# Two-layer macaron block on one core: weights laid out by the host, shared tiles moved forward, one product for the queries

## The chip, the cores and the metric

One core of one Trainium2 chip runs the whole program. The metric is device time in microseconds (us) of one execution, taken over several runs; the profile shows one more execution. The engines are named as in the profile: PE (TensorE), PEld (its weight loads), DVE (VectorE), ACT (ScalarE), POOL (GpSimd) and SP (SyncE, which only issues DMAs here).

## The reference, cut to what matters

Tokens are (2, 1024, 128) in f32. The block is FFN, attention, FFN, each on a layer norm of x and added to x:

```python
x = x + 0.5 * ffn(layernorm(x))
x = x + attn(layernorm(x))
x = x + 0.5 * ffn(layernorm(x))        # the same weights again
# attn, 16 heads of 8 columns
v = x @ w_v + v_b
q = (x @ w_q + q_b) @ w_k.T + k_b      # the keys are x itself
probs = softmax(causal(q @ x.T / sqrt(8)));  out = (probs @ v) @ c_proj_w + c_proj_b
# ffn: one shared expert and the 2 best of 7 routed ones, hidden width 352
expert(h, g, u, d) = (silu(h @ g.T) * (h @ u.T)) @ d.T
w = normalised top-2 of softmax(h @ wr.T + rb)
out = expert(h, sg, su, sd) + sum_e w[e] * expert(h, rg[e], ru[e], rd[e])
```

## The kernel before, in words

**Precision.** Every large product is made of three fp32r products: each operand is split into a high part (a copy to fp32r, by ACT) and a low part (operand minus high part, by DVE), and high x high, high x low and low x high are summed in PSUM. Weights need the same split (`wall` holds both parts of g, u and d for 8 experts; `small` those of attention).

**Weights.** g, u and d arrive as the reference has them, and both operands of a product must have the summed index on partitions. So PE transposes them: `weights_pe` (L1417) makes three transposes for one of 24 groups (8 experts x g, u, d) into a PSUM bank, `weights_hi_act` (L1454) copies the high part, `weights_lo_dve` (L1476) subtracts. Eleven groups (`TP_FIRST`) come ahead of the first tile, the other 13 one for each of the first 13 steps of the FFN. `weights_small_pe` (L1409) transposes w_k and the router's weights.

**Start.** 2048 tokens are four chunks (c) of 512. DVE makes statistics, POOL the reciprocal deviations (`norm_rstd_pool`), ACT the normalised rows z (`norm_z_act`), PE transposes them (`norm_tr_pe`, L548), ACT and DVE split (`norm_hi_act`, `norm_lo_dve`). `logits_pe` (L581) makes the router's logits. For each half (h) of the tokens, `router_dve` (L634) is a chain of 14 short DVE instructions that finds the two best experts, `places_pe` (L695) counts with two products, `places_dve` (L743) ends in `slots`, the rows to which POOL scatters each token (`sort_pool`, L1151: 16 indirect DMAs for a half, each followed by `pause_pool`, a memset). SP then reads tiles of sorted rows back (`rows_load_sp`, L1222): batch 0 to 2 (10 tiles) need the first half, batch 3 onward the second.

**FFN.** `ffn_pe`, `ffn_act` and `ffn_dve` (L961, L1016, L1125) walk 54 jobs of 128 tokens: 13 shared tiles (whose rows need no sorting), 38 routed tiles, 3 shared tiles. Step s makes the up products of job s, the transposes of job s-1 and the down products of job s-2. Each engine has one queue in program order. What else is done in a step is written in tables by hand (L2090 on): `FRONT_` ahead of the job's own work, `BETWEEN_` behind the up products or silu, `BEHIND_` at the end. `AWAKE` adds filler products (`busy_pe`) behind the up products of steps 0 and 1. POOL scatters the results (`scatter_pool`), and they are read back and mixed into x with the routing weights.

**Attention.** Queries take two products: `q1_pe` (x w_q), split with bias by `q1_act`/`q1_dve` (L1530, L1572), then `q_pe` (with w_k, L1519) and `q_act`/`q_dve`. Chunks 0 and 1 are done in steps 45 to 52 of the first FFN, chunks 2 and 3 inside the prologue of attention (`SECOND_PE`, `SECOND_DVE`, L1729), where DVE takes 54 maxima of score tiles (the ring) ahead of the first exponential. Then come 8 groups of 4 heads, and the second FFN.

```python
961 def ffn_pe(K, f):
963     for step in range(NQ + 2):
964         if f == 0 and TP_FIRST + step < NTP:
965             weights_pe(K, TP_FIRST + step)
...
974             if f == 0 or step > 0:
975                 up_pe(K, f, step, bases.get(step, 0))
```

Of the kernel before, what the change touches and what calls it, by code (L numbers as in the profile page):

```python
# [120 lines left out]
AWAKE = [{0: 2, 1: 3}, {}]  # L121
# [130 lines left out]
N_BANKS = (5, 4)  # L252
RING, SLOTS, O_BANK, END_BANK = (2, 5, 7, 3), (0, 1, 4), 6, 5
MID_N_BANK, Q1_BANK, Q_BANK, V_BANK = (7, 2, 0, 1), (3, 3, 4, 0), (7, 2, 6, 4), (7, 3, 1, 0)
# [3 lines left out]
TP_GROUPS = [(w, x) for x in range(EXPERTS) for w in ("g", "u", "d")]  # L258
NTP = len(TP_GROUPS)
TP_FIRST = 11  # L260
TP_BANK = [(0, 1, 2, 3, Z_BANK)[m % 5] if m < TP_FIRST else Z_BANK for m in range(NTP)]
# [6 lines left out]
TP_FREE = [max((p + 1 for p in range(m) if TP_BANK[p] == TP_BANK[m]), default=0) for m in range(NTP)]  # L268
# [3 lines left out]
N_CONST2 = 7  # L272
# [11 lines left out]
def place_memory(K, ctx):  # L284
# [19 lines left out]
    for w in ("q", "k", "v", "p"):  # L304
        for part in ("h", "l"):
            K.small[w + part] = sb(f"w{w}_{part}", [P, EMB], F32R)
# [5 lines left out]
    K.b_k = sb("b_k", [P, 1])  # L312
    K.b_v = sb("b_v", [P, EMB])
# [33 lines left out]
    with ExitStack() as s:  # L347
        zt = [sb(f"zt_{part}", [P, TOKENS], F32R, scope=s) for part in ("h", "l")]
        with ExitStack() as s2:
# [18 lines left out]
            with ExitStack() as s3:  # L368
                K.nat = {w: sb(f"nat_{w}", [P, EXPERTS, 3, EMB], scope=s3) for w in ("g", "u")}
                K.nat["d"] = sb("nat_d", [P, EXPERTS * HID + 32], scope=s3)  # L370
                K.nat_attn = sb("nat_attn", [P, 3 * EMB], scope=s3)
                K.nat_proj = sb("nat_proj", [P, EMB], scope=s3)
                K.nat_route = sb("nat_route", [P, P], scope=s3)
                rows = sb("rows", [32, 2, CHUNK], scope=s3)
                K.rows0, K.rows1 = rows[:, 0, :], rows[:, 1, :]
            with ExitStack() as s3:
# [3 lines left out]
                with ExitStack() as s4:  # L380
# [38 lines left out]
    with ExitStack() as s:  # L419
# [19 lines left out]
    K.ld = {n: sem(f"ld_{n}") for n in ("nat", "nat2", "small", "bias", "const", "out")}  # L439
# [3 lines left out]
    K.tp_pe, K.tp_hi, K.tp_lo = sem("tp_pe"), sem("tp_hi"), sem("tp_lo")  # L443
# [17 lines left out]
            ("q1", "q1f", "q1h", "q1l", "q", "qf", "qh", "ql", "v", "vev", "vb", "init",  # L461
             "ring", "taken", "mm", "sp", "ex", "mk", "pv", "oev", "vg", "ready", "nm", "rs", "vi", "og", "otr", "oh", "ol", "op", "bp", "xup")}
# [85 lines left out]
def norm_tr_pe(K, k, c):  # L548
# [10 lines left out]
    if c > 1:  # L559
# [456 lines left out]
def ffn_act(K, f):  # L1016
    for step in range(NQ + 1):
        if f == 0 and TP_FIRST + step < NTP:
            weights_hi_act(K, TP_FIRST + step)
# [131 lines left out]
def sort_pool(K, f, g):  # L1151
# [4 lines left out]
    if f == 0 or g % TT > 0:  # L1156
# [111 lines left out]
def start_sp(K):  # L1268
# [15 lines left out]
    e.dma_start(K.nat["d"][:, HID:EXPERTS * HID].rearrange("p (e i) -> p e i", i=HID), K.down_r.rearrange("e h i -> h e i"))\
     .then_inc(K.ld["nat2"], 16)
# [27 lines left out]
def start_act(K):  # L1313
# [4 lines left out]
    e.dma_start(K.nat_route[0:ROUTED, :], K.route_w).then_inc(K.ld["small"], 16)  # L1318
# [7 lines left out]
def start_pool(K):  # L1326
# [31 lines left out]
    e.memset(K.nat["d"][:, EXPERTS * HID:], 0.0).then_inc(K.consts2, 1)  # L1358
# [995 lines left out]
```

## Time and profile before

| | |
|---|---|
| median of 3 runs (lowest to highest) | 596.37 us (594.8 to 597.38) |
| the profiled execution | 592.31 us, its span 590.6 us |
| PE busy, share of the span | 543.8 us, 92% |
| DVE busy | 453.5 us, 77% |
| ACT busy | 331.0 us, 56% |
| POOL busy | 254.8 us, 43% |
| first FFN, silu of job 0 to silu of job 53 | 36.8 to 173.9 us |
| prologue of attention to its first exponential | 178.8 to 219.4 us |
| second FFN, silu of job 0 | from 453.4 us on |

The span runs from the first to the last instruction; the 1.7 us beside it lie around them. The timeline view gives start and duration of each instruction, and in brackets how long its engine had been idle before it and what released it. "Granted clock" (PEclk) is what the throttle allowed, as a share of full speed; the pace of the products themselves shows which of its two levels (1.2 or 2.4 GHz) PE runs at.

### The profile page before, as it was taken

Reading aid. Unit: us, or ns where it says so; the run is one execution under the profiler, and the core shown is the slowest. Engines: PE = TensorE matmul, PEld = TensorE weight load, DVE = VectorE, ACT = ScalarE, POOL = GpSimd, SP = SyncE. Lnnn points to the kernel's source line nnn. Section 1 sums busy time; section 2 is a strip of 40 time slices with the busy share of each in tenths; the row PEclk is TensorE's granted clock in tenths of the full one; section 3 lists DMA queues with packets and bytes.
Section 4 is the critical chain, followed back from the end, with each engine's and each line's share of the span. In section 5 each row is a group of like instructions: output and inputs, shape, how many; then the busy total and the mean of one; then the engine's idle time right before and its main releaser. Section 6 shows DMA issues by size and latency. Waiting matters only on the chain. (4 is left out here: it accounts for less than half of the span.)

```text
span 590.6 us, 11873 instructions
## 1 busy us (share of the span) xinstructions
PE 543.8 (92%) x3738; PEld 431.3 (73%) x3738; DVE 453.5 (77%) x1151; ACT 331.0 (56%) x701; POOL 254.8 (43%) x400
## 2 busy tenths in 40 slices
PE   1898999998895779999999999999999999999996
PEld 1778999997783546666666666666655889999995
DVE  3679868779548899797979797979564888777965
ACT  4454444446643527676767676768777434444543
POOL 7387856445342161111111212121236888864440
PEclk9999999999997989999999999999999999999997
DMA  9931435941563356222222222220000121341314
GB/s 244 290 83 38 122 80 145 234 126 48 162 197 110 114 155 162 82 87 83 88 86 84 90 80 86 86 88 10 4 2 24 32 78 52 101 110 59 107 38 113
DMA packets 46889, 58.74 MB, mean 99 GB/s; under 512 B 6183, under 2 KB 37678, under 8 KB 46062
## 3 DMA queue, kind: packets, MB, share of 16 engines
q1 hardware_dynamic: 38160, 46.77, 28.2%
q0 software_dynamic: 4480, 9.25, 4.9%
q10 hardware_dynamic: 4190, 1.98, 1.3%
q8 instruction: 33, 0.54, 0.4%
q14 instruction: 26, 0.21, 0.1%
HBM read 38.09 MB, written 28.00 MB: 112 GB/s over the span
## 5 line engine op out<-in xcount | busy, mean ns | idle before, releaser
L1771 DVE TENSOR_REDUCE mxp<-psum 128x1 f32<-128x512 f32 (+3 forms) x304 | 179.5, 655 | 30.3 <-PE psum L1617 29.4
L1830 ACT ACTIVATE probs<-psum 128x512 f32<-128x512 f32 (+1 forms) x304 | 155.1, 578 | 41.2 <-PE psum L1660 38.1
L1660 PE MATMUL psum<-queries,keys 128*128 128x512 f32 (+3 forms) x384 | 122.4, 381 | 0.5 <-DMA queries<-m_rows 0.3
L1617 PE MATMUL psum<-keys,queries 128*128 128x512 f32 (+1 forms) x304 | 115.3, 414 | 1.3 <-DVE mxp L1771 0.9
L1877 POOL TENSOR_SCALAR_AFFINE_SELECT probs<-probs 128x512 f32<-128x512 f32 x64 | 39.9, 634 | 175.5 <-ACT probs L1830 175.4
L1177 POOL DMA_INDIRECT y_rows<-ys,to_row x76 | 74.4, 979 | 81.4 <-DVE ys L1085 53.7
L996 ACT ACTIVATE silu<-psum 128x352 f32<-128x352 f32 x107 | 49.7, 464 | 102.6 <-PE psum L890 101.3
L1041 DVE TENSOR_TENSOR act<-silu,psum 128x352 f32<-128x352 f32 x107 | 55.5, 519 | 46.2 <-ACT silu L996 45.4
L1660 PEld LDWEIGHTS psum<-queries,keys 128*128 128x128 f32 x384 | 66.7, 190 | 26.7 <-ACT probs L1830 12.6
L1689 PE MATMUL psum<-probs,vg 128*32 128x512 f32 (+3 forms) x768 | 69.8, 491 | 0.4 <-POOL probs L1877 0.4
L1617 PEld LDWEIGHTS psum<-keys,queries 128*128 128x128 f32 x304 | 57.9, 193 | 15.0 <-DVE mxp L1771 4.8
L1047 DVE TENSOR_TENSOR at_l<-psum,at_h 128x384 fp32r<-128x384 f32 x108 | 59.5, 551 | 7.3 <-ACT at_h L1004 7.1
L906 PE MATMUL psum<-ident,act 128*128 128x128 f32 x324 | 53.7, 275 | 4.5 <-DVE at_l L1047 3.8
L1004 ACT CAST at_h<-psum 128x384 fp32r<-128x384 f32 x108 | 51.3, 475 | 9.1 <-PE psum L906 8.5
L888 PE MATMUL psum<-wall,zs_h 128*128 x152 | 54.0, 355 | 1.3 <-DVE zs_l L1072 1.0
L890 PE MATMUL psum<-wall,zs_l 128*128 x152 | 49.1, 323 | 0.0
L889 PE MATMUL psum<-wall,zs_h 128*128 x152 | 49.0, 323 | 0.0
L924 PE MATMUL psum<-wall,at_h 128*128 x228 | 47.6, 318 | 1.3 <-DVE ys L1085 1.3
L906 PEld LDWEIGHTS psum<-ident,act 128*128 128x128 f32 x324 | 40.9, 140 | 9.7 <-issue 4.4
L1689 PEld LDWEIGHTS psum<-probs,vg 128*32 128x32 f32 x768 | 21.1, 109 | 35.5 <-issue 21.7
L1154 POOL DMA_INDIRECT z_rows<-zrow,slots x32 | 31.2, 975 | 16.8 <-DVE slots L739 11.9
L924 PEld LDWEIGHTS psum<-wall,at_h 128*128 128x128 f32 x228 | 33.4, 190 | 2.9 <-issue 2.0
(260 smaller groups left out, 1020.5 us busy)
## 6 DMA issues: line engine op xcount, KB each, us to landing
z_rows<-q_stack SPq DMA_DIRECT2D x12, 682.5 KB, 5.2
keys<-q_stack SPq DMA_DIRECT2D x12, 512.0 KB, 10.3
keys<-k_stack SPq DMA_DIRECT2D x32, 128.0 KB, 6.3
queries<-q_stack SPq DMA_DIRECT2D x8, 512.0 KB, 6.0
zg_early<-z_rows SPq DMA_DIRECT2D x44, 65.0 KB, 1.9
yc<-y_rows SPq DMA_DIRECT2D x10, 256.0 KB, 3.9
zg_late<-z_rows SPq DMA_DIRECT2D x32, 65.0 KB, 2.1
k_stack<-zt_h SPq DMA_DIRECT2D x8, 256.0 KB, 3.0
```

The lines of the kernel that those rows point to most:

```text
L888: e.matmul(dst, zh, weight(K, base, hi, HID), start=True, stop=False)
L906: ins = e.transpose(bank(K, at_bank(f, q))[:, k * P:(k + 1) * P], K.act[:, q % 2, k * P:(k + 1) * P], K.ident[:, :])
L924: e.matmul(dst[:, 0:2 * EMB], K.at_h[:, q % 2, k * P:(k + 1) * P], weight(K, base, DN + 2 * k * EMB, 2 * EMB), start=(k == 0), stop=False, ...
L1004: e.copy(K.at_h[:, q % 2, :], bank(K, at_bank(f, q))[:, 0:ACOLS]).then_inc(s["hi"], 1)
L1041: e.tensor_tensor(act, silu, up, ALU.mult).then_inc(s["act"], 1)
L1047: e.tensor_tensor(K.at_l[:, q % 2, :], bank(K, at_bank(f, q))[:, 0:ACOLS], K.at_h[:, q % 2, :].bitcast(F32), ALU.subtract)\
L1177: e.indirect_dma_start(K.y_dram[f], bass.IndirectOffsetOnAxis(ap=K.to_row[:, j:j + 1], axis=0), K.ys[:, j % RING_Y, :], None).then_inc(K.y ...
L1617: ins = e.matmul(dst, K.queries[u][:, i * P:(i + 1) * P], K.keys[u][:, heads[0]:heads[-1] + 1, k0 * P:(k0 + nb) * P], start=True, stop=Tru ...
L1660: ins = e.matmul(slot(K, u, d, n)[:, m * (q1 - q0):(m + 1) * (q1 - q0)], K.keys[v][:, j, kt * P:(kt + 1) * P], K.queries[v][:, q0:q1], sta ...
L1689: ins = e.matmul(bank(K, O_BANK)[32 * j:32 * j + 32, q0 - half * CHUNK:q1 - half * CHUNK], K.vg[:, kt, j, :], probs_of(K, n)[:, j, :], sta ...
L1771: e.tensor_reduce(K.mxp[:, heads[0]:heads[-1] + 1, i, which], scores, AX.X, ALU.max).then_inc(K.A["taken"], 1)
L1830: e.activation(probs_of(K, product)[:, heads[0]:heads[-1] + 1, :], src, ACT.Exp, scale=SCALE).then_inc(K.A["ex"], 1)
```

## The change: what it does, and the diff

The host hands the weights over already transposed (and d padded with zero rows to 384), so the 24 groups of PE transposes and the two small ones are gone. The splits remain, in ten larger pieces: the 3 shared ones (352 or 384 elements a partition) on ACT and DVE ahead of the first tile; four (g and u of experts 1 to 3 and 4 to 7: 1056 and 1408 elements) with the high part on ACT and the low part **on POOL, ahead of the sort**; three (d, 896 elements each) on ACT and DVE in steps 0 to 3. The first tile follows the logits of chunks 0 and 1 at once. Transposes and splits of chunks 2 and 3, their logits, the places of the first half, and the second half's router (steps 6 and 7), places (step 10), segments and lists (up to step 15) move into the shared steps. The filler products and the pauses of the first FFN's sort are gone. w_q w_k^T is formed once by PE (`query_weights_pe`), with a combined bias, and queries take one product. SP loads the experts' weights with 6 DMAs instead of 14, in the same order.

```diff
-AWAKE = [{0: 2, 1: 3}, {}]
+AWAKE = [{}, {}]
...
+WEIGHTS = [(w, slice(0, 1)) for w in ("g", "u", "d")] + \
+          [(w, slice(x0, x1)) for w in ("g", "u") for x0, x1 in ((1, 4), (4, EXPERTS))] + [("d", k) for k in range(3)]
+SHARED_WEIGHTS = 3
+POOL_WEIGHTS = [3, 4, 5, 6]
+LATE_WEIGHTS = [7, 8, 9]
...
 def norm_tr_pe(K, k, c):
...
-    if c > 1:
+    if k == 0 and c == 3:
+        e.wait_ge(K.NS[k]["lo"], c)
+    elif c > 1:
         e.wait_ge(K.NS[k]["lo"], c - 1)
...
 def rows_tr_pe(K, f, b):
...
-        e.wait_ge(K.tp_lo, NTP)
+        e.wait_ge(K.w_lo, len(WEIGHTS) - len(POOL_WEIGHTS))
+        e.wait_ge(K.w_lo_pool, len(POOL_WEIGHTS))
...
 def ffn_pe(K, f):
...
-        if f == 0 and TP_FIRST + step < NTP:
-            weights_pe(K, TP_FIRST + step)
         if f == 0 and step == 0:
-            e.wait_ge(K.tp_lo, TP_FIRST)
+            e.wait_ge(K.w_lo, SHARED_WEIGHTS)
...
 def sort_pool(K, f, g):
...
-    if f == 0 or g % TT > 0:
+    if f == 1 and g % TT > 0:
         pause_pool(K, f == 1 and t < HALF)
...
+    e.dma_start(K.nat["g"][:, 0, :], K.gate_s).then_inc(K.ld["shared"], 16)
+    e.dma_start(K.nat["u"][:, 0, :], K.up_s).then_inc(K.ld["shared"], 16)
+    e.dma_start(K.nat["d"][:, :, 0, :], K.down_s).then_inc(K.ld["shared"], 16)
+    e.dma_start(K.nat["g"][:, 1:, :], K.gate_r).then_inc(K.ld["g"], 16)
+    e.dma_start(K.nat["u"][:, 1:, :], K.up_r).then_inc(K.ld["u"], 16)
+    e.dma_start(K.nat["d"][:, :, 1:, :], K.down_r).then_inc(K.ld["d"], 16)
...
+def query_weights_pe(K):
+    e = K.nc.tensor
...
+    e.matmul(bank(K, Y_BANK)[:, 0:EMB], K.nat_attn[:, 0:EMB], K.nat_attn[:, EMB:2 * EMB], start=True, stop=True,
+             skip_group_check=True)
+    e.matmul(bank(K, Y_BANK)[:, EMB:EMB + 1], K.nat_attn[:, EMB:2 * EMB], K.b_q[:, :], start=True, stop=True,
+             skip_group_check=True).then_inc(K.A["qk"], 1)
...
+def weights_lo(K, e, m, done):
+    w, src, hi, lo = (WEIGHTS[m][0],) + weights_of(K, m)
+    e.wait_ge(K.w_hi, m + 1)
+    if w != "d":
+        e.tensor_tensor(lo, src, hi.bitcast(F32), ALU.subtract).then_inc(done, 1)
+    else:
+        e.scalar_tensor_tensor(lo, src, 0.5, hi.bitcast(F32), ALU.mult, ALU.subtract).then_inc(done, 1)
...
 def q_pe(K, c):
...
-    three(K, e, bank(K, Q_BANK[c]), (K.small["kh"][:, :], K.small["kl"][:, :]), (K.q1_h[:, :], K.q1_l[:, :]))\
+    three(K, e, bank(K, Q_BANK[c]), (K.small["qh"][:, :], K.small["ql"][:, :]), (K.zt_h[1][:, cols], K.zt_l[1][:, cols]))\
         .then_inc(K.A["q"], 1)
-def q1_act(K, c):
...
-def q1_dve(K, c):
...
-SECOND_PE = {11: (("n_tr", 2),), 14: (("q1", 2),), 15: (("n_tr", 3),), 19: (("q1", 3),), 21: (("q", 2),),
-             25: (("q", 3),), 26: (("v", 2),), 28: (("v", 3),)}
+SECOND_PE = {11: (("n_tr", 2),), 15: (("n_tr", 3), ("q", 2)), 20: (("q", 3),), 21: (("v", 2),), 23: (("v", 3),)}
...
-FRONT_PE = {4: (("places", 1),), 45: (("n_tr", 0),), 46: (("q1", 0),), 47: (("n_tr", 1),), 48: (("q", 0), ("q1", 1)),
-            50: (("q", 1),), 51: (("v", 0),), 52: (("v", 1),)}
-BETWEEN_ACT = [{46: (("q1", 0),), 48: (("q", 0), ("q1", 1)), 50: (("q", 1),)}, {}]
+FRONT_PE = {9: (("places", 1),), 45: (("n_tr", 0),), 46: (("q", 0),), 47: (("n_tr", 1),), 48: (("q", 1),),
+            50: (("v", 0),), 51: (("v", 1),)}
+BETWEEN_ACT = [{0: (("hi0", 2),), 1: (("hi0", 3),), 46: (("q", 0),), 48: (("q", 1),)}, {}]
...
+FRONT_DVE = {4: (("segments", 0),), 5: (("lists", (0, 0)), ("lists", (0, 1)), ("lists", (0, 2)), ("lists", (0, 3))),
+             6: (("router", (1, 0)),), 7: (("router", (1, 1)),), 10: (("places", 1),), 11: (("segments", 1),),
+             12: (("lists", (1, 0)),), 13: (("lists", (1, 1)),), 14: (("lists", (1, 2)),), 15: (("lists", (1, 3)),)}
+BEHIND_DVE = [{0: (("query", 0),), 1: (("weights_lo", LATE_WEIGHTS[0]),), 2: (("weights_lo", LATE_WEIGHTS[1]),), 3: (("weights_lo", LATE_WEIGHTS[2]),), 13: (("small", 0),), 22: (("weights", 0),), 40: (("mix", 0),), 41: (("n_stats", 0),), 42: (("mix", 1),), 43: (("n_stats", 1),), 44: (("n_lo", 0),),
...
+BETWEEN_PE = [{0: (("tr0", 2),), 1: (("places", 0), ("tr0", 3)), 3: (("logits0", 2),), 4: (("logits0", 3),)}, {1: (("proj_tr", 2), ("proj_tr", 3)), 4: (("logits", 2), ("logits", 3)), 6: (("places", 1),)}]
+BETWEEN_DVE = [{0: (("lo0", 2),), 1: (("lo0", 3),)}, {4: (("router", (1, 0)),), 6: (("places", 1),)}]
...
         @block.gpsimd
         def _(e):
             start_pool(K)
             for c in range(NCH):
                 norm_rstd_pool(K, 0, c)
+            for m in POOL_WEIGHTS:
+                weights_lo(K, e, m, K.w_lo_pool)
             sort_part_pool(K, 0, 0)
             sort_part_pool(K, 0, 1)
...
+def laid_out(name, a):
+
+    if name == "attn_c_attn_w":
+        a = np.concatenate([a[:, 0:EMB].T, a[:, EMB:2 * EMB].T, a[:, 2 * EMB:]], axis=1)
+    elif name in ("ffn_sg", "ffn_su", "ffn_wr"):
+        a = a.T
+    elif name in ("ffn_rg", "ffn_ru"):
+        a = a.transpose(2, 0, 1)
+    elif name in ("ffn_sd", "ffn_rd"):
+        rows = np.moveaxis(a, -1, 0)
+        padded = np.concatenate([rows, np.zeros_like(rows[0:3 * P - HID])])
+        a = np.moveaxis(padded.reshape((3, P) + rows.shape[1:]), 0, 1)
+    return np.ascontiguousarray(a)
```

## Rows read from the trace of the kernel before

**Rows 1.** Windows: length, busy us of each engine, granted clock, DMA share, GB/s
```profile
15.00:20.00 5.00, 4.92 (x23) 4.95 (x24) 1.65 (x6) 3.32 (x9) 1.23 (x2) 1.00 1.05 280
...
34.60:37.90 3.30, 3.30 (x12) 2.29 (x11) 1.19 (x3) 2.24 (x3) 2.97 (x5) 1.00 0.15 45
37.90:45.00 7.10, 7.10 (x51) 6.05 (x50) 6.04 (x21) 3.16 (x7) 6.44 (x10) 1.00 0.11 38
...
158.00:166.00 8.00, 6.46 (x37) 5.89 (x36) 3.84 (x8) 3.57 (x9) 2.11 (x2) 0.79 0.59 183
```

**Rows 2.** Timeline, ACT and DVE, 14.6 to 25.2 us: normalised rows, the first half's router chain
```profile
14.66 3.41 ACT L531 ACTIVATE zrow<-x,mr_neg,rstd 128x128 f32<-128x128 f32 x8
...
18.73 0.22 DVE L628 TENSOR_TENSOR r_log<-psum,rb_row 128x64 f32<-128x64 f32 x1 [3.20 <-PE psum L596]
...
21.89 0.22 DVE L672 TENSOR_TENSOR r_sel<-r_c,r_m 128x64 bf16<-128x64 f32 x1
...
24.99 0.17 DVE L739 CAST slots<-d_slot 128x16 int32<-128x16 f32 x1
```

**Rows 3.** Timeline, ACT: a cast from SBUF of 512 elements
```profile
150.80 0.62 ACT L1539 CAST q_h<-q_f 128x512 fp32r<-128x512 f32 x1
```

**Rows 4.** Groups by form, POOL: times run, busy us, mean ns, idle before
```profile
L1164 POOL MEMSET idle<- 128x384 bf16 x68 | 29.5, 434 | 0.0
L1556 POOL TENSOR_TENSOR v_all<-v_all,b_v 128x128 f32<-128x128 f32 x16 | 7.2, 481 | 9.2 <-ACT v_all L1546 9.1
L2075 POOL TENSOR_TENSOR x<-x,b_p 128x512 f32<-128x512 f32 x4 | 4.9, 1266 | 0.0
```

**Rows 5.** Source L1779, DVE: shortest, median and longest ns of eight
```profile
L1779 DVE TENSOR_TENSOR mm_hl<-nmax,mm_hl x8: 191/193/1195, 214.1 to 418.5; 128x32 fp32r<-128x32 f32 x8
```

**Rows 6.** Timelines of DVE and of POOL, 212.7 to 215.3 us
```profile
214.08 1.20 DVE L1779 TENSOR_TENSOR mm_hl<-nmax,mm_hl 128x32 fp32r<-128x32 f32 x1
...
212.74 2.48 POOL L2075 TENSOR_TENSOR x<-x,b_p 128x512 f32<-128x512 f32 x2
```

**Rows 7.** Timeline, ACT: silu of jobs 3 and 12, first FFN
```profile
45.09 0.46 ACT L996 ACTIVATE silu<-psum 128x352 f32<-128x352 f32 x1 [0.49 <-PE psum L890]
...
70.82 0.47 ACT L996 ACTIVATE silu<-psum 128x352 f32<-128x352 f32 x1 [0.48 <-PE psum L890]
```

**Rows 8.** Timeline, ACT: silu of shared jobs 4, 9, 51 and 53, second FFN
```profile
468.80 0.46 ACT L996 ACTIVATE silu<-psum 128x352 f32<-128x352 f32 x1 [0.38 <-PE psum L890]
...
484.50 0.46 ACT L996 ACTIVATE silu<-psum 128x352 f32<-128x352 f32 x1 [0.60 <-issue]
...
575.39 0.46 ACT L996 ACTIVATE silu<-psum 128x352 f32<-128x352 f32 x1 [1.20 <-PE psum L890]
...
580.01 0.46 ACT L996 ACTIVATE silu<-psum 128x352 f32<-128x352 f32 x1 [1.48 <-PE psum L890]
```

**Rows 9.** Timeline, ACT: silu of jobs 46, 50 and 53, first FFN
```profile
149.72 0.46 ACT L996 ACTIVATE silu<-psum 128x352 f32<-128x352 f32 x1 [0.31 <-PE psum L890]
...
164.84 0.46 ACT L996 ACTIVATE silu<-psum 128x352 f32<-128x352 f32 x1 [3.12 <-PE psum L890]
...
173.90 0.46 ACT L996 ACTIVATE silu<-psum 128x352 f32<-128x352 f32 x1 [1.08 <-PE psum L890]
```

**Rows 10.** Timeline, DVE: in the prologue of attention
```profile
199.37 0.68 DVE L1577 TENSOR_TENSOR q_l<-q_f,q_h 128x512 fp32r<-128x512 f32 x1
...
201.32 0.69 DVE L1771 TENSOR_REDUCE mxp<-psum 128x4 f32<-128x512 f32 x1 [0.67 <-PE psum L1617]
```

**Rows 11.** Timeline: POOL's last scatter of the sort, SP's and PE's batch 3
```profile
76.87 0.96 POOL L1154 DMA_INDIRECT z_rows<-zrow,slots  x1 [0.16 <-issue]
...
79.32 0.88 SPq L1238 DMA_DIRECT2D zg_early<-z_rows  x2
...
90.94 0.40 PE L947 MATMUL psum<-ident,zg_early 128*128 128x128 f32 x2
```

**Rows 12.** The page, DMA issues: count, KB each, median us to landing
```profile
zg_early<-z_rows SPq DMA_DIRECT2D x44, 65.0 KB, 1.9
```

More of the change, by code:

```diff
@@ L251 @@
 AT_BANKS = (5, 7)
-N_BANKS = (5, 4)
+N_BANKS = (5, 4, 6, 6)
 RING, SLOTS, O_BANK, END_BANK = (2, 5, 7, 3), (0, 1, 4), 6, 5
[L254 to L261, printed above, removed]
+MID_N_BANK, Q_BANK, V_BANK = (7, 2, 0, 1), (7, 2, 6, 4), (7, 3, 1, 0)
+WEIGHTS = [(w, slice(0, 1)) for w in ("g", "u", "d")] + \
[3 more added lines that the diff above has]
+LATE_WEIGHTS = [7, 8, 9]
 RING_LAST = RING0[LAST] + RINGN * (GROUPS - 1)
@@ L267 @@
 R_BANKS = [[R_BANK, R_BANK], [EARLY_BANKS[0], R_BANK]]
-TP_FREE = [max((p + 1 for p in range(m) if TP_BANK[p] == TP_BANK[m]), default=0) for m in range(NTP)]
 N_CONST = 6
-N_CONST2 = 7
+N_CONST2 = 6
 N_SPARES = 4
@@ L303, in place_memory @@
     K.small = {}
-    for w in ("q", "k", "v", "p"):
+    for w in ("q", "v", "p"):
         for part in ("h", "l"):
@@ L435, in place_memory @@
     K.psum = ctx.enter_context(K.nc.psum_tensor("psum", [P, 8, CHUNK], F32))
-    K.ld = {n: sem(f"ld_{n}") for n in ("nat", "nat2", "small", "bias", "const", "out")}
+    K.ld = {n: sem(f"ld_{n}") for n in ("shared", "g", "u", "d", "small", "bias", "const", "out")}
     K.ld_x = [sem(f"ld_x{b}") for b in range(BATCH)]
@@ new lines, in small_sources, with weights_of @@
+def small_sources(K):
+    return [("v", K.nat_attn[:, 2 * EMB:]), ("p", K.nat_proj[:, :])]
+def weights_of(K, m):
+    w, part = WEIGHTS[m]
+    wall = K.wall[:, :].rearrange("p (x c) -> p x c", c=WCOLS)
+    if w != "d":
+        hi, lo = (GH, GL) if w == "g" else (UH, UL)
+        return K.nat[w][:, part, :], wall[:, part, hi:hi + HID], wall[:, part, lo:lo + HID]
+    down = wall[:, :, DN:].rearrange("p x (k a m) -> p x k a m", a=2, m=EMB)
+    if m < SHARED_WEIGHTS:
+        return K.nat[w][:, :, 0, :], down[:, 0, :, 0, :], down[:, 0, :, 1, :]
+    return K.nat[w][:, part, 1:, :], down[:, 1:, part, 0, :], down[:, 1:, part, 1, :]
@@ new lines, in weights_hi_act @@
+def weights_hi_act(K, m):
+    e, w = K.nc.scalar, WEIGHTS[m][0]
+    src, hi, _ = weights_of(K, m)
+    if m < SHARED_WEIGHTS:
+        e.wait_ge(K.ld["shared"], 16 * 3)
+    else:
+        e.wait_ge(K.ld[w], 16)
+    if w == "d":
+        e.activation(hi, src, ACT.Copy, scale=0.5).then_inc(K.w_hi, 1)
+    else:
+        e.copy(hi, src).then_inc(K.w_hi, 1)
+def weights_lo(K, e, m, done):
+    w, src, hi, lo = (WEIGHTS[m][0],) + weights_of(K, m)
+    e.wait_ge(K.w_hi, m + 1)
+    if w != "d":
+        e.tensor_tensor(lo, src, hi.bitcast(F32), ALU.subtract).then_inc(done, 1)
+    else:
+        e.scalar_tensor_tensor(lo, src, 0.5, hi.bitcast(F32), ALU.mult, ALU.subtract).then_inc(done, 1)
@@ L1856, in attn_act @@
     e = K.nc.scalar
-    e.wait_ge(K.A["ready"], 1)
+    e.wait_ge(K.A["ready"], 2)
     for c in range(2, NCH):
@@ L2142, in late_act @@
         norm_z_act(K, 2, c)
+    elif step == "hi0":
+        norm_hi_act(K, 0, c)
+    elif step == "weights":
+        weights_hi_act(K, c)
     elif step == "tanh":
@@ L2173, in late_dve @@
         norm_z_dve(K, 2, c)
+    elif step == "lo0":
+        norm_lo_dve(K, 0, c)
+    elif step == "query":
+        query_weights_dve(K)
+    elif step == "small":
+        weights_small_dve(K)
+    elif step == "weights_lo":
+        weights_lo(K, K.nc.vector, c, K.w_lo)
     elif step == "norm_lo":
@@ L2235, in _ @@
             logits_pe(K, 0, 0, 1)
[L2236 to L2245 removed]
+            query_weights_pe(K)
             ffn_pe(K, 0)
```

220 lines of the change are left out of this document (62 added, 158 removed).

## Prediction

> **What bounds the kernel now.** I read the windows first, then the timeline of the first 80 us engine by engine, then the waits. Up to 34.6 us no tile is computed: PE transposes weights and makes logits, ACT and DVE split. From the first tile on PE is nearly always busy [rows 1], except between the first FFN and attention (6.46 of 8 us in 158 to 166 us). So the change can pay in three places: the start, that passage, and the prologue of attention, where DVE is the bound. From the first loop of attention to the end nothing that it edits is on the path, and I carry the sum of the three through unchanged. A change of under 0.5% (3.0 us) can't be told from none here.
>
> **Start: what goes.** The 24 transpose groups go; eleven stood ahead of the tiles, and the filler products of steps 0 and 1 as well. If nothing else came, PE would reach the first up products right behind the logits, whose results DVE takes up at 18.73 us [rows 2], against 34.6 us.
>
> **Start: what comes on POOL.** ACT ends the normalised rows at 14.66 + 3.41 = 18.07 us [rows 2]. Three shared casts come ahead (1.15 us, at under 0.4 us each after the cast of 512 in 0.62 us [rows 3]), so 19.2. The first large cast (1056 elements, 1056 x 0.62 / 512 = 1.28) ends at 20.5, all four by 25.2. POOL subtracts the low parts. Its nearest rows are a two-input product of 128 elements, 0.48 us, and of 512, 1.27 us [rows 4]: 2.04 ns an element. So 1056 cost 2.4 us, 1408 cost 3.1, all four 11.0 us, without a gap because ACT is ahead. DVE meanwhile runs the router's chain (18.73 to 22.11 us) and the places (slots ready at 25.16) [rows 2], short instructions, nearly all with two SBUF inputs.
>
> Do the two engines get in each other's way? L1779, a DVE subtraction of 32 elements with both inputs in SBUF, takes 191 to 193 ns, and once 1195 [rows 5]. That once, it starts at 214.08 and ends at 215.28, just when POOL's x + b_p ends (212.74 + 2.48 = 215.22) [rows 6]. It stood for the rest of POOL's instruction. I take this as the rule for the chain: each DVE instruction with two SBUF inputs that meets a running POOL subtraction waits for its end. Four waits are needed (L659, L664 with L665, L667, L672), as many as there are POOL instructions, since POOL's next is queued when DVE's one has passed. POOL ends at 20.5 + 11.0 + 0.6 for DVE's turns = 32.1, the router at 32.35 instead of 22.11, 10.2 us late, and the slots at 35.4 instead of 25.16. From below: no waits, nothing; from above: 11 us, all of POOL.
>
> The Trainium skill, SBUF — State Buffer, "Who interferes with whom", speaks against the change: a DVE instruction with two SBUF inputs and a GpSimd instruction that reads SBUF share one read interface, and the loser is held for the whole instruction. By it all four waits come; by the one row alone I would know only of one, and with one wait (2.4 us) the sum would be some 7.8 us better. The trace agrees as far as it goes, 1195 ns against 193.
>
> **Who waits for DVE.** `places_dve` is queued on DVE ahead of job 0's product. PE makes up 0 and 1 by 24 us and then stands at `places_pe`. From 35.4 on: job 0's product 0.5, low part of chunk 2 0.7, transposes of chunk 3 1.1, of job 0 0.6, up of job 2 1.7, transposes of job 1 0.6, down of job 0 1.9, up of job 3 1.4 and silu's wait 0.4, since PE comes out of a pause and its instructions start about every 0.28 us, as in 34.6 to 37.9 us, not every 0.14 as behind it [rows 1]. Silu of job 3 falls on 44.3, against 45.09 [rows 7]: **0.8 us** gained. Without the waits the slots come at 26.7 (PE reaches the places at 24), and 9.5 us would be gained.
>
> **Steps 3 to 12.** Before, nine jobs take 70.82 - 45.09 = 25.7 us [rows 7], each with a transpose group. Without one a shared job takes (580.01 - 575.39) / 2 = 2.31 us [rows 8]. But logits of chunks 2 and 3, router, places and segments of the second half now lie in these steps. The second FFN has the same work in jobs 4 to 9, 15.7 us for five [rows 8], 4.15 above 5 x 2.31. For the segments and lists of the first half I add 1.5 (below 0, above 3). 9 x 2.31 + 4.15 + 1.5 = 26.4: **0.7 lost**. The late weights (896 elements, three on ACT and DVE, about 1 us each) lie beside PE's slow steps 0 to 3.
>
> **Between FFN and attention.** Jobs 46 to 53 take 173.90 - 149.72 = 24.2 us [rows 9]. Gone are six products of 512 columns, four ACT casts (0.62 [rows 3]) and two DVE subtractions (0.68). Where q and q1 met in step 48, 2.6 us of ACT stood ahead of the transposed activations; 1.3 remain. Followed job by job the silus come 0.5, 1.4, 2.7 and at last 3.3 us earlier. Bounds: 1.3 (one pair of casts) and 4.0 (24.2 less seven jobs at 2.31 and 4.0 us of other products). I take **3.3**.
>
> **Prologue.** DVE is busy nearly throughout; it loses two subtractions of 0.68 and the 0.67 us for which it waits behind the second step of the queries [rows 10]. With v moved five places forward, POOL's x + b_p ends ahead of L1779, another 1.0 [rows 5]. Together **3.0**, bounds 1.4 and 3.7.
>
> **Covered.** The query weights cost PE two small products, about 0.5 us, in the time in which it waits anyway; if the waits on DVE don't come they cost 0.5. SP has fewer, larger DMAs, and clears the keys behind the row loads as before.
>
> **Sum.** 0.8 - 0.7 + 3.3 + 3.0 = 6.4 us. The profiled execution took 592.31 us (span 590.6 and 1.7 around it), which gives 585.9; it lies 4.1 below the median of the runs, 596.37. I predict from the median: **590.0 us**.
>
> **Rivals.**
> 1. *DVE isn't held.* Only one row shows the hold, and other two-input instructions beside short POOL work took their usual time. Then 9.5 - 0.7 - 0.5 + 3.3 + 3.0 = 14.6: 581.8 us. Chance 0.15.
> 2. *Some waits.* DVE gets two instructions through at each turn: two POOL instructions fewer in the way, some 5 us more: 585 us. Chance 0.12.
> 3. *The second half's sort is late.* Its places move from step 5 to step 10: five jobs at 2.86 [rows 7] behind 53.5 (last scatter at 76.87, 15 at 1.56 ahead of it [rows 11]), so 67.7. Without pauses 16 scatters take 1.12 each (0.96 and a gap of 0.16): 85.6. SP loads 1.5 later, as 79.32 stands to 77.83 [rows 11], two issues 0.9, landing 1.9 [rows 12]: 89.9, and batch 3 is wanted at 90.9. One us is left. If the scatters without the memset (0.43 [rows 4]) need 1.56 all the same, rows come 6 us late and the gain is 0.4: 596 us. Chance 0.08.
> 4. *Slower: PE stays at its lower level.* In 15 to 20 us PE was busy 4.92 of 5 us with narrow products at the slow pace though 1.00 was granted, and it rose only behind fillers [rows 1]. Now there are none, and PE has a pause ahead. At twice the interval a shared job takes about 4.2 us, 1.9 more; from four jobs on the whole gain is lost, over jobs 3 to 12 it is 19: 603 us. Against it: up products of 352 columns follow one another closely as soon as jobs run. Chance 0.07.
>
> **The numbers.** My forecast has 0.58, of which 0.09 gain under 3 us (the bounds of the steps at their worst). Faster by over 0.5%: 0.49 + 0.15 + 0.12 = 0.76; within: 0.09 + 0.08 = 0.17; slower: 0.07. The range runs from 580 (rival 1 and a little) to 595 (the lower bounds, most of rival 3); rival 4 and the edges are left out.
>
> **What would show it.** In the changed profile: L659 to L672 with durations of 2 to 3 us and POOL's four subtractions at 2.4 and 3.1; the first half's slots at 35 us (27 in rival 1); silu of job 3 near 44; jobs 3 to 12 in 26.4; jobs 46 to 53 in 21; first exponential 6 us earlier; no wait on batch 3 (one of 6 us in rival 3). Small router instructions at 0.22 us throughout would prove the start wrong; shared jobs of 4 us, rival 4.

## The result and the profile after

The changed kernel took 615.49 us (median of four runs, 612.52 to 617.52); the kernel before took 596.88 in the runs beside it. Ratio 1.031, 95% interval 1.0247 to 1.0373: **slower by 18.6 us**, where 6.4 us of gain were forecast. The profiled execution has a span of 615.7 us against 590.6.

The page of the changed kernel, its head, TensorE's busy tenths and granted clock in 40 slices, and the shares of the chain that ended last:

```profile
span 615.7 us, 11594 instructions
...
PE   1473946999899588999999999999999899989996
...
PEclk9877877999999697999999999999999989999998
...
PE 63%; DVE 13%; issue 10%; another core or an unknown queue 5%; POOL 3%; ACT 3%; DMA 2%; SPq 1%; DVEq 0%; POOLq 0%
```

PE has holes in slices 2 to 7, up to 108 us. 15% of the chain is time for which the profile can name no cause ("issue" and "another core or an unknown queue"; 5% in e10 below, which runs almost the same program without the trouble). Where it lies is shown by silu, ACT's first instruction of each job. The changed kernel, timeline of ACT, jobs 3, 4, 5, then 12 and 13, then 46 and 53:

```profile
41.48 0.46 ACT L1000 ACTIVATE silu<-psum 128x352 f32<-128x352 f32 x1 [0.61 <-PE psum L892]
44.64 0.46 ACT L1000 ACTIVATE silu<-psum 128x352 f32<-128x352 f32 x1 [1.49 <-issue]
55.72 0.46 ACT L1000 ACTIVATE silu<-psum 128x352 f32<-128x352 f32 x1 [7.37 <-remote]
...
80.30 0.46 ACT L1000 ACTIVATE silu<-psum 128x352 f32<-128x352 f32 x1 [3.16 <-issue]
97.23 0.46 ACT L1000 ACTIVATE silu<-psum 128x352 f32<-128x352 f32 x1 [9.40 <-remote]
...
175.26 0.47 ACT L1000 ACTIVATE silu<-psum 128x352 f32<-128x352 f32 x1 [0.31 <-PE psum L892]
...
196.17 0.47 ACT L1000 ACTIVATE silu<-psum 128x352 f32<-128x352 f32 x1 [1.57 <-issue]
```

Job 3 came 3.6 us earlier than before [rows 7]. Jobs 3 to 12 then took 38.8 us instead of 25.7, and job 13 another 16.9 (before 3.8). Jobs 46 to 53 took 20.91 against 24.2 [rows 9], as forecast. The lost time lies in two stretches, and in both POOL scatters without a pause: 37.75 to 58.4 us and 75.33 to 95.3 us, one scatter each 1.26 us. The changed kernel, waits in 43 to 60 us (engine, line waited for, us in total, times, longest):

```profile
ACT silu L1000 <- remote: 7.4, 1, 7.4
PEld psum L908 <- issue: 7.1, 2, 5.5
PE psum L908 <- issue: 5.1, 1, 5.1
ACT at_h L1008 <- remote: 4.4, 2, 2.8
POOL z_rows L1154 <- issue: 3.7, 12, 0.3
DVE act L1043 <- issue: 3.6, 1, 3.6
DVE at_l L1049 <- issue: 2.5, 2, 1.8
```

PE, ACT and DVE all stand, though the instructions they depend on have ended; I call this a stall. POOL alone goes on. The second FFN, whose code is unchanged, lost 4.9 us too (jobs 1 to 53 in 126.8 instead of 121.9).

The start went nearly as forecast. The changed kernel, DVE's router chain (each line has a number two higher than in the kernel before), POOL's four subtractions and its first scatter:

```profile
19.91 2.33 DVE L659 TENSOR_TENSOR r_sel<-r_c,zrow 128x64 bf16<-128x64 f32 x1
22.28 3.10 DVE L661 SCALAR_TENSOR_TENSOR r_w<-r_sel,r_log 128x64 f32<-128x64 bf16 x1
...
25.66 2.08 DVE L666 TENSOR_TENSOR r_c<-r_w,r_p 128x64 f32<-128x64 f32 x1
27.66 3.12 DVE L667 TENSOR_TENSOR r_d<-r_m,r_p 128x8 f32<-128x8 f32 x1
...
34.37 0.17 DVE L741 CAST slots<-d_slot 128x16 int32<-128x16 f32 x1
```
```profile
19.71 5.59 POOL L1463 TENSOR_TENSOR wall<-nat_g,wall 128x1056 fp32r<-128x1056 f32 x2 [3.62 <-ACT wall L1456]
25.24 5.52 POOL L1463 TENSOR_TENSOR wall<-nat_u,wall 128x1056 fp32r<-128x1056 f32 x2
37.75 1.22 POOL L1154 DMA_INDIRECT z_rows<-zrow,slots  x1 [6.99 <-issue]
```

### The profile page after: what moved, and what is told of

Its sections match the earlier page's. It is cut to its first block, busy times and chain, and to the rows that moved or that the text cites. A ratio compares the mean times of both kernels' runs of the same rounds, so it can differ in the third digit from the quotient of the medians.

```text
span 615.7 us, 11594 instructions
## 1 busy us (share of the span) xinstructions
PE 538.0 (87%) x3646; PEld 424.5 (69%) x3646; DVE 452.3 (73%) x1129; ACT 323.9 (53%) x678; POOL 252.6 (41%) x371
## 4 chain that ended last, share of the span: by engine, by line
PE 63%; DVE 13%; issue 10%; another core or an unknown queue 5%; POOL 3%; ACT 3%; DMA 2%; SPq 1%; DVEq 0%; POOLq 0%
PE psum L1631 12%; PE psum L1588 11%; PE psum L1660 10%; PE psum L890 4%; PE psum L892 4%; PE psum L908 4%; PE psum L929 4%; PE psum L891 4%; PE psum L932 2%; DVE mxp L1741 2%; PE psum L1591 2%; DVE at_l L1049 1%; POOL z_rows L1154 1%; PE psum L1616 1%
## 5 line engine op out<-in xcount | busy, mean ns | idle before, releaser
L908 PE MATMUL psum<-ident,act 128*128 128x128 f32 x324 | 55.9, 283 | 15.0 <-issue 5.5
L890 PE MATMUL psum<-wall,zs_h 128*128 x152 | 55.1, 363 | 9.9 <-issue 9.1
L1008 ACT CAST at_h<-psum 128x384 fp32r<-128x384 f32 x108 | 51.3, 475 | 16.9 <-PE psum L908 6.9
L891 PE MATMUL psum<-wall,zs_h 128*128 x152 | 50.1, 329 | 0.0
L1660 PEld LDWEIGHTS psum<-probs,vg 128*32 128x32 f32 x768 | 21.1, 109 | 35.6 <-issue 21.4
L1154 POOL DMA_INDIRECT z_rows<-zrow,slots x32 | 31.5, 984 | 33.0 <-DVE slots L741 16.9
L890 PEld LDWEIGHTS psum<-wall,zs_h 128*128 128x128 f32 x152 | 29.6, 195 | 10.6 <-issue 10.3
```

The costliest lines, as they stand in the source:

```text
L890: e.matmul(dst, zh, weight(K, base, hi, HID), start=True, stop=False)
L891: e.matmul(dst, zh, weight(K, base, lo, HID), start=False, stop=False)
L908: ins = e.transpose(bank(K, at_bank(f, q))[:, k * P:(k + 1) * P], K.act[:, q % 2, k * P:(k + 1) * P], K.ident[:, :])
L1660: ins = e.matmul(bank(K, O_BANK)[32 * j:32 * j + 32, q0 - half * CHUNK:q1 - half * CHUNK], K.vg[:, kt, j, :], probs_of(K, n)[:, j, :], sta ...
```

## The experiments

Sixteen kernels, and two programs run once more, in five sets. The kernels of one set share a chip and the runs of the kernel before; each set had another chip (its number is in the table; that of the result isn't on record). All results first, because their order by set turned out to be the finding. "Stalls" means that PE, ACT or DVE stands for 3 us or more, with no releaser that the trace can name, while POOL scatters; the longest such stand in a trace marked "no" is 2.7 us.

| set, chip | kernel before, us | run | us | ratio, 95% interval | stalls |
|---|---|---|---|---|---|
| result | 596.9 | changed kernel | 615.5 | 1.031, 1.025 to 1.037 | yes |
| 1, chip 7 | 593.1 | e1 pauses back | 595.9 | 1.0039, 1.0007 to 1.0071 | no |
| 1, chip 7 | | e2 before, no pauses | 593.6 | 1.0002, 0.997 to 1.0034 | no |
| 1, chip 7 | | e3 lock off | 591.1 | 0.9963, 0.9931 to 0.9995 | no |
| 1, chip 7 | | e4 short pauses | 591.3 | 0.997, 0.9932 to 1.0007 | no |
| 2, chip 2 | 600.9 | e5 lock off, no pauses | 613.7 | 1.0207, 1.0158 to 1.0257 | yes |
| 2, chip 2 | | e6 pauses in first half | 612.8 | 1.0188, 1.0124 to 1.0251 | second half |
| 2, chip 2 | | e7 each fourth pause | 616.4 | 1.0247, 1.0184 to 1.031 | yes |
| 2, chip 2 | | e8 before, 20 pauses ahead | 628.9 | 1.0456, 1.0389 to 1.0522 | yes |
| 3, chip 4 | 594.3 | e9 before, 20 memsets ahead | 593.9 | 0.9984, 0.9948 to 1.0021 | no |
| 3, chip 4 | | e10 changed, 20 memsets ahead | 591.4 | 0.9957, 0.9929 to 0.9985 | no |
| 3, chip 4 | | e11 lock off, short pauses | 589.0 | 0.9903, 0.987 to 0.9937 | no |
| 3, chip 4 | | e12 and fillers | 589.5 | 0.9899, 0.9865 to 0.9934 | no |
| 4, chip 6 | 593.4 | e13 20 memsets behind | 592.2 | 0.9979, 0.9946 to 1.0012 | no |
| 4, chip 6 | | e14 10 memsets | 591.7 | 0.9927, 0.9897 to 0.9956 | no |
| 4, chip 6 | | e15 40 memsets | 591.7 | 0.9944, 0.99 to 0.9988 | no |
| 4, chip 6 | | e16 wait alone | 591.3 | 0.9981, 0.994 to 1.0021 | no |
| 5, chip 15 | 595.1 | e17 changed kernel again | 614.3 | 1.0319, 1.0276 to 1.0362 | yes |
| 5, chip 15 | | e18 = e2 again | 624.4 | 1.0494, 1.0458 to 1.0529 | yes |

**Set 1: pauses and lock, one at a time.** "Lock" is short for POOL's subtractions holding DVE. e1, the changed kernel with the pauses back; e2, the kernel before with the opposite edit:

```diff
-    if f == 1 and g % TT > 0:
+    if f == 0 or g % TT > 0:
```

> The changed kernel with the pauses between the scatters of the first FFN back (a memset of 0.43 us behind each of the 32), nothing else undone. Theory A (without pauses POOL's scatters hold up the other engines; the two stretches of stalls, 45 to 59 us and 77 to 98 us, go): the first FFN's jobs 3 to 13 take the 29.5 us of the kernel before instead of 55.8, and the time is 585 to 593 us, near 589. Rival B (the stalls come of what else was changed: rows that land late, the layout's transfers, the missing fillers' clock): the stalls stay, 608 us or more. A time between, 595 to 605 us, would say that both take part.

> The kernel before without the pauses between the scatters of the first FFN, nothing else changed. Theory A: the same stalls appear in it while POOL scatters, 610 to 622 us. Rival B: the pauses were only time of POOL, whose sort has slack: 590 to 598 us, no change that can be told. Rival C (as in the prediction, the sort ends earlier by 16 x 0.6 us and feeds the first routed tiles): up to 3 us faster.

e3 is e1 with the four subtractions moved from POOL to DVE, in BEHIND_DVE[0] (POOL_WEIGHTS, renamed MID_WEIGHTS, remains for ACT's casts):

```diff
-            for m in POOL_WEIGHTS:
-                weights_lo(K, e, m, K.w_lo_pool)
...
+ 4: (("weights_lo", 3),), 5: (("weights_lo", 4),), 8: (("weights_lo", 5),), 9: (("weights_lo", 6),),
```

> As the kernel with the pauses back, and the low parts of the four large weights taken from POOL and put on DVE, behind its work of jobs 4, 5, 8 and 9. Theory A with the lock (POOL's 11.1 us of subtractions held DVE's router chain, for which PE stood 8.7 us): against the kernel with the pauses back 5 to 9 us faster, near 582 us, the four router operations back at 0.23 us. Rival D (the 8.7 us are covered by something else that is late, or the four subtractions of some 1.2 us now make DVE late in jobs 4 to 9): within 2 us of it.

e4 is e1 with a memset of 32 columns in each pause of the first FFN:

```diff
-        pause_pool(K, f == 1 and t < HALF)
+        pause_pool(K, f == 1 and t < HALF, 32 if f == 0 else PAUSE)
```

> As the kernel with the pauses back, with a memset of 32 columns instead of 384 in each pause of the first FFN, so that a scatter comes each 1.25 to 1.35 us instead of 1.57, with POOL's wait for its own memset kept. Theory A1 (it is the rate of the scatters that holds the others up): the stalls come back in good part, 600 us or more. Theory A2 (it is that POOL never stands still between two scatters; any wait of its own frees the others): as with the full pause, within 2 us of it.

e1 had no stalls, but at 595.9 us it was not the 589 of theory A, and above its 593. e2 had none either: on this evidence the pauses protect nothing in the kernel before. I took that at first for an effect of the program. e4 was 4.7 us faster than e1, where the theory without stalls (A2) had at most 2. e3, DVE's router chain and slots, then POOL's first scatter:

```profile
20.30 0.23 DVE L659 TENSOR_TENSOR r_sel<-r_c,zrow 128x64 bf16<-128x64 f32 x1
20.56 0.23 DVE L661 SCALAR_TENSOR_TENSOR r_w<-r_sel,r_log 128x64 f32<-128x64 bf16 x1
...
26.29 0.17 DVE L741 CAST slots<-d_slot 128x16 int32<-128x16 f32 x1
```
```profile
27.45 1.22 POOL L1153 DMA_INDIRECT z_rows<-zrow,slots  x1 [10.49 <-DVE slots L741]
```

Without POOL's subtractions the held instructions are back at 0.23 us and the slots come 8.1 us earlier than in the changed kernel. That shows the hold. The kernel gained 4.8 us against e1 (595.93 to 591.11), a little less than the 5 to 9 expected: job 3 came 8.0 us earlier than in e1 (34.60 against 42.59), but DVE makes the four subtractions now, PE waits for it, and at job 13 1.2 us of the 8.0 are left (70.99 against 72.14).

**Set 2: what the stalls need.** e5 is e3 without the pauses of the first FFN. e6 and e7 change the condition in the changed kernel, e8 adds pauses to e2 (in this order):

```diff
-    if f == 1 and g % TT > 0:
+    if f == 0 and t < HALF or f == 1 and g % TT > 0:
```
```diff
-    if f == 1 and g % TT > 0:
+    if f == 0 and t % 2 == 0 and r == 0 or f == 1 and g % TT > 0:
```
```diff
+            for _ in range(20):
+                pause_pool(K)
             sort_part_pool(K, 0, 0)
```

> The kernel with the lock off (low parts of the four large weights on DVE), without the pauses in the first FFN: the changed kernel with the lock alone undone. So far the pauses' absence cost 20 us in the changed kernel and nothing in the kernel before, at the same spacing of the scatters (1.26 us), and a scatter each 1.27 us with a short wait between stalled nobody. Theory E (the stalls need scatters without a wait between them at a place in time that the lock brought about: POOL's sort then runs 11 us later against the other engines): with the sort again beginning near 27 us no stall, 588 to 594 us. Theory F (they need scatters without a wait and something else of the changed kernel: its program or its layout in SBUF): the stalls stay, 604 us or more.

> The changed kernel with the pauses in the first half of the first FFN's sort alone. If each half's stalls come of its own scatters: the stretch at 45 to 59 us is free, the one at 77 to 98 us stays with some 12 us, and the time is 602 to 609 us. If the second stretch was only a consequence of the first: 593 to 599 us.

> The changed kernel with one pause behind each fourth scatter of the first FFN. If the stalls build up over a row of scatters and one wait of POOL's clears them: within 3 us of the kernel with all pauses (596). If each scatter without a wait costs its share: some three quarters of the 20 us stay, 609 us or more.

> The kernel before without the pauses, and 20 of them in a row ahead of the first half's sort, so that its scatters begin some 11 us later (near 37 to 38 us), as in the changed kernel. Theory E (place in time): the stalls appear, 604 us or more. Theory F (the changed program or layout): no stall, 593 to 600 us, the later sort being covered in part.

All four stalled. The most useful is e6. Its waits in 43 to 64 us (first half, with pauses) and in 66 to 84 us (second half, without):

```profile
ACT silu L1000 <- PE psum L892: 9.3, 6, 1.9
ACT silu L1000 <- issue: 3.0, 2, 1.5
```
```profile
ACT silu L1000 <- remote: 5.4, 1, 5.4
...
DVE act L1043 <- issue: 4.1, 1, 4.1
```

Within one execution the half with pauses runs (jobs 3 to 11 in 21.9 us; in e10, which didn't stall, 21.4), the half without stalls (job 11 to 13 in 27.2 us, e10 8.1). Its time, 612.8 us, lies above the 602 to 609 expected; the kernel before took 600.9 there. One pause in four (e7) doesn't protect. e8 did not do what I meant: its pauses ended before the slots were ready, so the scatters began at 26.56 us, as in e2 at 26.43, and at the same pace. Yet e2 had run free and e8 stalled. I looked for the cause in POOL's program, the only difference between the two kernels, and passed over the other one, the chip.

**Sets 3 and 4: the place in the program.** Short memsets of 2 columns, which only move what stands behind them in POOL's program: e9 in e2 ahead of the sort; e10, e14 and e15 in the changed kernel ahead of POOL's subtractions (20, 10, 40); e13 behind the sort.

```diff
+            for i in range(20):
+                e.memset(K.idle[:, 2 * i:2 * i + 2], 0.0).then_inc(K.rested, 1)
+                K.rests += 1
```

> The kernel before without the pauses, and 20 memsets of 2 columns in POOL's program ahead of the sort: as many instructions more as in the kernel with 20 pauses ahead of it (which stalled, 1.046, although its scatters began at 26.56 us as they did without, 26.43, and came as fast), but POOL done with them by 20 us and standing for some 6 us before the first scatter. Theory P (what decides whether scatters without a wait stall the others is where in POOL's program they stand): the stalls appear, ratio to the kernel before 1.02 or more. Theory Q (it is that POOL was at work right up to the first scatter): no stall, ratio 0.995 to 1.005.

> The changed kernel with 20 memsets of 2 columns in POOL's program ahead of its four subtractions, in time in which POOL stood. Theory P: the stalls change, by several us up or down, or go (ratio 1.00 to 1.02, or 1.04 and more). Theory Q: they stay as they are, ratio 1.027 to 1.037.

> The changed kernel with the 20 memsets of 2 columns in POOL's program behind both halves of the sort instead of ahead of it. Ahead of it they took all stalls away (0.9957). If it is the place of the scatters in POOL's program (or what POOL did ahead of them): nothing changes for the 32 scatters, ratio 1.025 to 1.037, both stretches of stalls there. If it is what stands behind them or the length of the program: the stalls go, 0.993 to 1.003.

> The changed kernel with 10 memsets of 2 columns ahead of POOL's subtractions (20 took the stalls away). If any shift or any such work ahead is enough: 0.993 to 1.003. If the place matters in steps: the ratio can be that of the changed kernel, 1.02 or more, at this number.

> The changed kernel with 40 memsets of 2 columns ahead of POOL's subtractions. If such work ahead is enough: 0.993 to 1.003 as with 20. If the place matters in steps: the stalls may be back, 1.02 or more; with 10 and 20 and 0 that gives the pattern.

e16 puts a wait between the scatters of the changed kernel, on a semaphore long met (`elif f == 0: e.wait_ge(K.numbered, 1)`):

> The changed kernel with a wait between the scatters of the first FFN for a semaphore that has long been met, and no memset. If a wait in the instruction frees the others (the scatters take it in with no instruction between): no stalls, 0.993 to 1.003. If it needs an instruction of another kind, or POOL's stand for its own memset: as the changed kernel, 1.025 to 1.037.

None stalled, whatever the number or the place: a theory that needs a place can't hold when every place is right. What they share is the chips of sets 3 and 4. Because nothing stalled there or in set 1, e16 and e4 say nothing about what in a pause protects: POOL's wait, the memset, or the wider spacing of the scatters (1.56 us instead of 1.26).

**Set 5: the same programs again.** e17 is the changed kernel, e18 is e2, not a letter different:

> The changed kernel as it is, once more. Theory G (chips differ: on some, scatters without a wait between them hold up all engines, on others not; every shift of the program did nothing): where the kernel before takes 592 to 595 us, no stalls and a ratio of 0.990 to 1.001; where it takes 596 us or more, the stalls and 1.02 to 1.04. Theory H (the program: the place of POOL's instructions in it): 1.025 to 1.037 on any chip.

> The kernel before without the pauses, once more (1.0002 the first time). Theory G: where the kernel before takes 592 to 595 us, 0.997 to 1.003 again; where it takes 596 us or more, stalls, 1.02 to 1.05. Theory H: 0.997 to 1.003 on any chip.

e18 settles that it isn't the program: the same one gave 1.0002 in set 1 and 1.0494 here. Nor does it change from run to run: e2 took 591.4 to 595.6 us in ten runs, e18 623.6 to 627.2 in six. e2, then e18, timeline of ACT (jobs 0 and 1) and of POOL (one scatter of the row):

```profile
37.30 0.46 ACT L996 ACTIVATE silu<-psum 128x352 f32<-128x352 f32 x1
40.69 0.46 ACT L996 ACTIVATE silu<-psum 128x352 f32<-128x352 f32 x1 [0.62 <-PE psum L890]
...
43.25 0.96 POOL L1154 DMA_INDIRECT z_rows<-zrow,slots  x1 [0.31 <-issue]
```
```profile
36.51 0.46 ACT L996 ACTIVATE silu<-psum 128x352 f32<-128x352 f32 x1
47.71 0.46 ACT L996 ACTIVATE silu<-psum 128x352 f32<-128x352 f32 x1 [5.86 <-remote]
...
43.18 0.96 POOL L1154 DMA_INDIRECT z_rows<-zrow,slots  x1 [0.30 <-issue]
```

POOL scatters at the same times in both; only the others' stands differ: job 1 comes 7.0 us later. So the removed pauses cost the kernel before 29.3 us here (595.1 to 624.4) and nothing in set 1. My bound for theory G (596 us for the kernel before) was a little off: it took 595.1. Over the six sets of runs it took 593.1, 593.4 and 594.3 where nothing stalled, and 595.1, 596.9 and 600.9 where scatters without pauses did.

There is a mark in the profile. The DMA issues of e2 and of e18 (the last number is the median time to landing):

```profile
z_rows<-zrow,slots POOLq DMA_INDIRECT x32, 2.4
```
```profile
z_rows<-zrow,slots POOLq DMA_INDIRECT x32
z_rows<-zrow_late,slots POOLq DMA_INDIRECT x32
```

In the seven traces with stalls the profile finds no landing of these scatters; in the other twelve experiments and in the kernel before it does (2.3 to 2.7 us). But it is no mark of the stalls themselves. In the same seven traces the landing is also missing for the scatters of the second FFN (`zrow_late`, the second line), which keep their pauses, and in e6 for the first half's, beside which nobody stalled. All seven come from the three sets that stalled, so the mark may belong to the chip; the kernel before has only one trace, whose chip isn't on record. What it means I can't say.

**The better kernels.** e11 joins e3 and e4. e12 adds the fillers of the kernel before (`AWAKE = [{0: 2, 1: 3}, {}]`, into bank AT_BANKS[0]).

> Lock off and the short pauses (32 columns) in the first FFN together. Each gave some 4 us against the kernel with the full pauses. With both, the first half's sort ends near 48 us instead of 54.7 and 59.6, SP's row loads, its clearing of keys and the results' loads come earlier, and the stands at jobs 12, 20 and 40 of the kernel with the lock off (some 10 us in all) go: ratio to the kernel before 0.978 to 0.990. Rival: the stands have another cause, or DVE's four subtractions in jobs 4 to 9 are what is late: 0.994 to 0.998, no better than either.

> As the kernel with lock off and short pauses, with the fillers of the kernel before back (2 and 3 pairs of 512-column products in jobs 0 and 1, into bank 5). If the granted clock of the first stages (0.84 at 15 to 37 us, 0.91 at 60 to 98 us with the lock off, 1.00 in the kernel before) is what is lost: 2 to 5 us faster than without them and 1.00 shown there. Rival: the clock falls in stands that the fillers don't reach, and they lie ahead of the router's products: within 1 us, or up to 2 us slower.

Both are 1.0% faster than the kernel before (5.3 and 4.7 us in the medians) and some 2 us faster than e10 of the same set. That just misses what I expected (at most 0.990). In e11's trace PE doesn't wait for rows, but 2.2 and 1.6 us for DVE around jobs 11 to 13 (job 12 at 68.8 us; before 70.8), and ACT waits 3.7 us for the results. The fillers change nothing in the time (0.9899 against 0.9903). In the traces the granted clock at 15 to 37 us is 0.92 with them and 0.76 without, and job 46 comes 2.9 us earlier, but the second FFN takes 3.3 us more (125.7 against 122.4), which stays unexplained. Neither was run on a chip that stalls.

## Why the prediction was wrong

**The removed pauses: the step that failed.** The prediction had them only in rival 3, as time of POOL's, and gave the removal no cost. On the chips of three of six sets of runs a row of scatters without them stalls PE, ACT and DVE. The trace of before could not show it, since it holds no row of scatters without a pause; the bound "from above" for that edit was never set. On the chip of set 5 the same edit alone costs the kernel before 29.3 us, more than the 25 us of the miss. By which path the scatters stall the others stays open. The changed kernel with all its pauses was not run on such a chip, so its time there stays open; e6 shows for the first half that they help it.

The rest is judged by e10, the nearest to the changed kernel without stalls (0.9957, a gain of 2.6 us against the forecast 6.4). Timeline of ACT, jobs 3, 12, 13, 46 and 50:

```profile
42.04 0.46 ACT L1000 ACTIVATE silu<-psum 128x352 f32<-128x352 f32 x1 [0.63 <-PE psum L892]
...
66.64 0.47 ACT L1000 ACTIVATE silu<-psum 128x352 f32<-128x352 f32 x1 [1.49 <-PE psum L892]
71.50 0.47 ACT L1000 ACTIVATE silu<-psum 128x352 f32<-128x352 f32 x1 [2.96 <-PE psum L892]
...
151.90 0.46 ACT L1000 ACTIVATE silu<-psum 128x352 f32<-128x352 f32 x1 [0.31 <-PE psum L892]
...
164.70 0.47 ACT L1000 ACTIVATE silu<-psum 128x352 f32<-128x352 f32 x1 [2.72 <-PE psum L892]
```

- **The hold on DVE: right.** POOL 11.1 us (forecast 11.0), four waits of 2.08 to 3.12, slots at 34.5 (35.4). Two of the four fell on other instructions of the chain than I named (L657 and L665 in the numbers of the kernel before; L667 and L672 weren't held). One odd row [rows 5] had the rule in it. The Trainium skill, SBUF — State Buffer, "Who interferes with whom", has a DVE instruction with two SBUF inputs contend with a GpSimd instruction that reads SBUF; the trace agrees, 2.33 us against 0.23 in e3. Rivals 1 and 2 fall.
- **From the slots to job 3: mis-sized.** I gave it 8.9 us, at the slow pace throughout; it took 6.9 in the changed kernel and 7.2 in e10. Job 3 came 3.0 us earlier in e10, not 0.8.
- **Steps 3 to 12: mis-sized.** 24.6 us in e10, not 26.4: 1.1 gained, where 0.7 were to be lost. The next job, 13, gave the 1.1 back (4.9 us, before 3.8).
- **Jobs 46 to 53: right.** 20.9 us in the changed kernel, 20.9 forecast.
- **"SP ... clears the keys behind the row loads as before": wrong.** The first scatter fell on 35.80 us (26.15 before), and what stands on SP's queue behind it moved. The timeline of SP in e10, clearing of the keys and first loads of the results, then SP's wait ahead of these loads (90 to 150 us), then landing of the clearing and of POOL's result scatters (95 to 140 us):

```profile
107.92 3.69 SPq L1393 DMA_DIRECT2D keys<-q_stack  x8
131.23 2.04 SPq L1249 DMA_DIRECT2D yc<-y_rows  x4
```
```profile
SPq L1245 <- DMA y_rows<-ys,to_row: 19.4, 2, 19.0
```
```profile
keys<-q_stack SPq DMA_DIRECT2D x8, 512.0 KB, 12.9
...
y_rows<-ys,to_row POOLq DMA_INDIRECT x19, 6.4
```

Before these stood at 100.12 and 128.75. The loads weren't held up by SP's queue: SP stood 19.0 us until POOL's result scatters had landed. The last scatter that they need (the 22nd) was issued at 124.58, earlier than before (126.30), but the loads followed it 6.7 us later, before 2.5. The clearing, 4 MB, had moved by 7.8 us to where it runs beside that scatter. Around job 41 ACT now waits 3.8 us for yc, DVE behind ACT, and PE 3.3 us for DVE. From job 13 to job 46 e10 took 80.4 us, the kernel before 75.2 (149.72 - 74.57): **5.2 us lost that my sum didn't have**, 3.8 of them at job 41 and 1.5 in jobs 13 to 17, whose cause stays open. I had followed the late slots to the tiles, but not along SP's queue to the clearing and to what it then meets. That the clearing delays the landing is argued from these rows; no run has it moved alone.
- **Prologue, 3.0: mis-sized, and ahead of it a part of the 3.3 was given back.** The last routed job, 50, came at 164.70, before at 164.84 [rows 9]. On its results hang the second half's norms, so PE's transposes for them stood at 190.59, before at 190.48: of the 3.3 us of jobs 46 to 53 some 1 us, gained behind job 50, ends in this wait. Behind the transposes 2.2 us were gained, not 3.0 (the first exponential at 217.31, before at 219.35, where 6 us were forecast). So from job 46 to the first exponential 4.2 us were gained of the 6.3 in the sum. From job 53 to the second FFN's job 1 it was only 0.5 us (283.7 against 284.2). A term counts only from the wait that ends last behind it.
- **Rival 3:** scatters without pauses need 1.26 us, not 1.12: the gap is 0.30, not 0.16. **Rival 4,** the lower clock: it was lower (0.945 in the mean against 0.980), but shared jobs took 2.3 us in e10, not 4. A part came with the stands (0.74 in 40 to 100 us in e18, 1.00 in e2), a part without them (0.83 up to 40 us in e10, before 1.00), and the fillers, which raised it, brought no time. The rival's 603 us doesn't follow from its own 19 us, which give 609.

## What to carry to other kernels

An instruction that looks idle (a memset of 0.43 us behind each scatter) may be there for the others. If the trace of before doesn't contain the state without it, its removal has no upper bound and wants one experiment of its own before anything else is changed. And repeat the decisive kernel on another chip before building a theory: here sixteen kernels differed by program and by chip at once, and the programs got the blame. When an early producer moves by 9 us, follow each in-order queue behind it, SP's too, to its last item, and ask what its transfers then run beside.

## What the runs showed that I had not expected

- Scatters from POOL without a wait between them (1.26 us each) hold up PE, ACT and DVE for 3 to 9 us at a time on some chips (three sets of runs) and not at all on others (three), with the same program. No chip is known to have had two sets of runs, so whether it is the chip, a condition of it or how the program was loaded there, and by which path, is open. The traces speak against starved instruction loads: in 26 to 46 us e2 and e18 moved the same packets on the two instruction queues (1 and 2), and in the changed kernel none lands when the engines go on at 55 to 59 us.
- Code that keeps its pauses was slower there too: the second FFN took 126.8 to 129.2 us from job 1 to 53 in six of the seven traces with stalls (123.6 in e18), and 121.8 to 125.7 in those without. Whether that comes of the removed pauses or of the chip isn't shown: no trace of the kernel before is known to be from a chip that stalls.
- Full pauses aren't free in the changed kernel either: e1 took 4.7 us more than e4 (595.9 against 591.3), whose short ones let a scatter through each 1.27 us.
